# Weighted sums of the first query group taken one step later, in a fused attention and mixture-of-experts kernel

## The chip, the core and the metric

One core of one Trainium2 chip. The metric is device microseconds for one execution of the whole kernel. The engines are TensorE (PE in the profile), VectorE (DVE), ScalarE (ACT), GpSimd (POOL) and SyncE (SP, which issues DMAs here). Each runs its own list of instructions in order; semaphores tie the lists together.

## What is computed

The input `x` is 2 x 1024 tokens of width 256, the context 2 x 77 rows of width 256. The first half is a cross-attention in which every head of 16 has its own query part of a projected row, and keys and values come from context rows chosen by an argmax; the second half is a top-2 mixture of 8 experts.

```python
qp = einsum('bld,ed->ble', q, Wq);  scores = einsum('bld,bmd->blm', qp, kv)
mem = take_along_axis(kv, argmax(scores)[..., None], axis=1)
mk, mv = split(einsum('bld,ed->ble', mem, Wkv), 2)
attn = softmax(einsum('bhld,bmd->bhlm', qh, mk) * scale)
x = x + einsum('bld,ed->ble', heads(einsum('bhlm,bmd->bhld', attn, mv)), Wc)
# then, on layernorm(x): probs = softmax(x @ router_w.T); top 2 of 8 experts
h = einsum('td,eid->tei', x, w1);  y = h[..., 512:] * silu(h[..., :512])
out = x + einsum('tei,ehi,te->th', y, w2, combine)
```

Since `mem` repeats the 77 context rows, the kernel works with the 77 distinct keys and weights each by how often it was chosen (`cc`, and `vc` = values times counts).

## The kernel before

The tokens are 16 tiles of 128, in four groups of four tiles (`NH` = 4, `u` is the group). After a head that normalises x, projects queries and picks the context rows, the attention runs over the groups, and each group has four steps `s` (`STEPS`), one for four heads, written as eight slots `k` (`SLOTS`). For one step:

- TensorE, `scores_turned(u, s)` (L1405): the logits with keys on partitions, less the row maxima, into PSUM banks 0 to 3 (16 products). It waits for the exponential of the step before, which reads these banks.
- ScalarE, `exps(u, s)` (L623): the exponential of these banks into `pT`, which has two buffers.
- TensorE, `sums(u, s)` (L1421): the product of `pT` with `vc` into one bank (4 for groups 0 to 2): weighted sums and denominators. It waits for the exponential of its own step and, since there is one bank, for the normalisation of the step before. Ahead of it `fill(4, 2)` issues two products whose result nobody reads (L1273), in group 0 only.
- ScalarE, `sums_out` (L630): a copy to `uT`; TensorE, `turn_sums` (L1429): the transpose back; VectorE, `normalise` (L875, L877): reciprocal and product into `on`, which releases the next `sums`.

In between, for the group to come, TensorE computes `logits` (L1365), two per step, with tokens on partitions, and VectorE reduces each to maxima (`maxima`, L861). In groups 1 to 3 they have one pair of banks, so a logit waits for the reduction of the one before. `ahead(u, k)` names the logit that a slot of group u works on; `LEAD` = 2 puts it ten slots ahead. `turn_maxima` (L1382) and `maxima_turned` (L616) turn a whole group's maxima. `counts(1)` (L1342, L1345) counts the picks of the second batch element, and `picked`, `replaced`, `spread` on VectorE build the keys `kb` and values `vc` of it, which groups 2 and 3 need. From group 1 on, a slot also holds the steps of the group before: `turn_heads`, `combine`, `residual`, router and ranks.

A second stream runs under it. The expert weights are 48 tiles of 128 x 512. For each, a cast to the high part (`high`, L602, on ScalarE, in numbers per slot from `HIGH_SLOT`; the last few on GpSimd, L496) and the low part as a difference in bfloat16 on GpSimd (`splits`, L502) into `low`, a staging tile with `LR` = 3 buffers, 128 KB each. SyncE stores each to DRAM (`keep_lows`, L389) and loads them back when the queries' space is free (`inner_lows`, L410; the loads for experts 0 and 1 in group 1, 2 and 3 in group 2, 4 to 7 in group 3). Three waits tie the stream:

```python
if n >= 2:
    act.wait_ge(low_ok, n - 1)                        # cast of tile n: tile n-2 is subtracted
...
if n >= LR:
    pool.wait_ge(low_out[n % LR], 16 * (n // LR))     # tile n's difference: tile n-3 is stored
...
sp.wait_ge(low_ok, n + 1)                             # store of tile n
sp.dma_start(lows[n], low[:, n % LR, :]).then_inc(low_out[n % LR], 16)
```

SyncE's list is in order too. Between its stores stand other transfers, at places that `high_before(u, k)` computes from `HIGH_SLOT`: it is the number of tiles that ScalarE has cast before slot k of group u. `keep_until(n)` stores all tiles below n. `HIGH_ACT`, 45 before, is how many tiles ScalarE casts. GpSimd's list holds all 48 differences, and then the first four `gather`s (L525), which bring the rows of the first expert blocks; TensorE's `turn_rows` (L1618) waits for the first of them, and the expert products (L1633, L1642, L1649) follow. 39 blocks are worked in turn. The end of SyncE's list around it:

```python
keep_until(high_before(3, 0)); inner_lows(4); inner_lows(5)
keep_rows(1)
inner_lows(6); inner_lows(7)      # the last waits for scores(3, 3)
keep_until(NC)
sp.wait_ge(g_in[0], 16)           # the first gather
outer_lows(0); outer_lows(1)
```

Of the kernel before, what the change touches and what calls it, by code (L numbers as in the profile page):

```python
# [25 lines left out]
NH = T // HT  # L26
# [31 lines left out]
STEPS = 4  # L58
# [6 lines left out]
WC_AT = ((5, 5, 5, 5), (5, 5, 5, 5), (5, 5, 5, 7), (5, 7, 5, 7))  # L65
LEAD = 2
KB = 8
CHAIN = 7

HIGH_HEAD = (0, 0, 2, 3, 2)  # L70
HIGH_SLOT = ((2, 2, 2, 1, 2, 1, 1, 1), (2, 2, 2, 2, 2, 1, 1, 1), (2, 2, 2, 2, 2, 1, 1, 1))
HIGH_FIRST = sum(HIGH_HEAD)
# [3 lines left out]
def ahead(u, k):  # L76

    w, n = divmod(SLOTS * (u + 1) + k + LEAD, SLOTS)
    return (w, n) if w < NH else None


# [26 lines left out]
def build(nc, x, ctxT, Wq, WqT, WkvT, Wc, WcT, routerT, w, out):  # L108
    rows = nc.dram_tensor("rows", [(T + 1) * P, RW], F32).ap()
    lows = nc.dram_tensor("lows", [NC, P, CW], BF16).ap()  # L110
    with ExitStack() as ctx:
# [457 lines left out]
        def _(act):  # L569
# [107 lines left out]

            for u in range(NH - 1):
                for k in range(SLOTS):
                    if k % 2 == 0:  # L680
                        exps(u, k // 2)
                    if k == 7:
                        maxima_turned(u + 1)
                    if k % 2 == 1:
                        sums_out(u, k // 2)
                    if u >= 1 and k in (1, 2):
                        heads_turned(u - 1, k - 1)
                    if u == 2 and k == 1:
                        weights(0)
                        x2_normal(0, (0, 1))  # L690
                    if u == 2 and k == 3:
                        x2_normal(0, (2, 3))
                    high(HIGH_SLOT[u][k])

# [65 lines left out]
        def _(dve):  # L760
# [360 lines left out]

            for u in range(NH - 1):
                v = u - 1
                for k in range(SLOTS):
# [8 lines left out]
                    if k % 2 == 0 and k:  # L1133
                        normalise(u, k // 2 - 1)
                    if u == 0 and k == 2:
                        picked(1)
                    if u == 0 and k == 3:
                        replaced(1)
                    if u == 0 and k == 4:
                        spread(1)  # L1140
                    if u >= 1 and k == 3:
# [125 lines left out]
        def _(pe):  # L1267
# [140 lines left out]
            def sums(u, s):  # L1408
# [6 lines left out]
                else:  # L1415
                    pe.wait_ge(ql_ok, 2 * NH)
                if u == 0:
                    fill(4, 2)
                pe.wait_ge(ex_ok, n + 1)
# [131 lines left out]

            for u in range(NH - 1):
                for k in range(SLOTS):
# [21 lines left out]
                    if u >= 1 and k == 0:  # L1575
                        turn_sums(v, STEPS - 1)
                    if u == 0 and k == 1:
                        counts(1)
                    if u >= 1 and k == 3:
# [176 lines left out]
```

## Time and profile before

| | |
|---|---|
| median of 3 runs | 355.68 us (355.19 to 356.42) |
| profiled execution: time, span | 353.84 us, 352.0 us |
| mean granted TensorE clock | 0.986 |
| TensorE busy | 323.9 us (92% of the span) |
| VectorE, ScalarE, GpSimd busy | 192.2, 211.8, 193.1 us |
| groups 0, 1, 2 (scores to scores) | 50.34 to 71.31 to 95.76 to 121.37 us |
| first expert product | 141.64 us |

The span goes from the first to the last instruction; the execution's own time has what lies around it as well. The groups are the stretches from the first score product of one group to that of the next. Busy shares are over the whole span, most of which is the experts' loop; the attention groups fill 50 to 141 us.

### The profile page before, as it was taken

The numbers are of one execution on the slowest core, as the hardware profiler recorded it, in microseconds if no ns is written. First come the engines' busy times: TensorE is split into PE (matmuls) and PEld (weight loads), VectorE is DVE, ScalarE is ACT, GpSimd is POOL, SyncE is SP. The second block draws the span as 40 slices with busy tenths as digits, with TensorE's granted clock in tenths as the row PEclk, the third lists the DMA queues.
The fourth block names the chain that finished last, engine by engine and source line by source line (L and its number), as shares of the span: only waits on it lengthen the run. The fifth ranks groups of instructions, "written<-read, shape, count | busy, mean of one in ns | idle before, by whom it ended". The sixth has DMA issues, their size and how long they took to land.

```text
span 352.0 us, 7569 instructions
## 1 busy us (share of the span) xinstructions
PE 323.9 (92%) x2324; PEld 221.7 (63%) x2325; DVE 192.2 (55%) x648; ACT 211.8 (60%) x380; POOL 193.1 (55%) x215
## 2 busy tenths in 40 slices
PE   7998989998988899999999999999999999999940
PEld 3855544454444545786767777777777777777730
DVE  3996865636769799787884333333333333333310
ACT  1927427876788693856655556666556665566620
POOL 3401637876868783656766555545555554555330
PEclk9999999999999999999999999999999999999995
DMA  8999535825254377925234432333332333333221
GB/s 239 373 386 387 189 108 163 242 78 181 76 164 151 124 226 242 299 64 153 47 92 64 73 63 49 59 52 53 61 59 34 58 61 61 61 48 51 39 30 15
DMA packets 35690, 43.77 MB, mean 124 GB/s; under 512 B 3312, under 2 KB 28272, under 8 KB 35664
## 3 DMA queue, kind: packets, MB, share of 16 engines
q1 hardware_dynamic: 27088, 32.58, 27.9%
q0 software_dynamic: 7488, 10.39, 18.3%
q10 hardware_dynamic: 1088, 0.46, 0.6%
q8 instruction: 15, 0.25, 0.3%
q14 instruction: 11, 0.09, 0.1%
HBM read 27.49 MB, written 15.93 MB: 123 GB/s over the span
## 4 chain that ended last, share of the span: by engine, by line
PE 67%; POOL 9%; DVE 7%; DMA 6%; issue 6%; ACT 3%; SPq 0%; POOLq 0%; ACTq 0%; DVEq 0%
PE ps L1633 28%; PE ps L1642 15%; POOL low L502 6%; DMA lows<-low 5%; PE ps L1649 5%; PE ps L1332 3%; PE ps L1458 2%; PE ps L1273 2%; PE ps L1618 2%; PE ps L1421 2%; PE ps L1319 2%; POOL ex L535 2%; PE ps L1405 1%; DMA out_x<-xn,idx 1%; ACT pT L623 1%
## 5 line engine op out<-in xcount | busy, mean ns | idle before, releaser
L1633 PE MATMUL ps<-W,kb 128*128 x312 | 95.9, 429 | 0.0
L502 POOL TENSOR_TENSOR low<-raw,W 128x256 bf16<-128x256 f32 x96 | 67.0, 731 | 39.4 <-ACT W L602 31.1
L542 POOL DMA_INDIRECT out_x<-xn,idx x39 | 61.8, 1585 | 46.3 <-ACT xn L721 25.4
L525 POOL DMA_INDIRECT X<-rows,idx x39 | 39.1, 1002 | 47.7 <-ACT xn L721 34.9
L1633 PEld LDWEIGHTS ps<-W,kb 128*128 128x128 f32 x312 | 56.0, 189 | 12.4
L1195 DVE TENSOR_TENSOR kb<-ps,mT 128x512 fp32r<-128x512 f32 x39 | 27.0, 692 | 58.6 <-ACT mT L733 58.5
L1191 DVE TENSOR_TENSOR uT<-uT,ps 128x512 f32<-128x512 f32 x39 | 26.8, 686 | 45.9 <-PE ps L1633 44.3
L1633 PE MATMUL ps<-W1lo,kT 128*128 x156 | 47.2, 384 | 0.0
L721 ACT ACTIVATE xn<-ps,X 128x256 f32<-128x256 f32 x39 | 18.5, 474 | 36.0 <-PE ps L1642 31.7
L711 ACT CAST kb<-ps 128x256 fp32r<-128x256 f32 x39 | 14.5, 373 | 38.0 <-PE ps L1618 34.7
L861 DVE TENSOR_REDUCE mx<-ps 128x8 f32<-128x616 f32 x32 | 25.3, 795 | 20.3 <-PE ps L1365 20.3
L623 ACT ACTIVATE pT<-ps 77x2048 f32<-77x2048 f32 x16 | 29.9, 1871 | 5.1 <-PE ps L1405 5.0
L602 ACT CAST W<-raw 128x512 fp32r<-128x512 f32 x45 | 26.8, 616 | 7.7 <-POOL low L502 7.6
L1642 PE MATMUL ps<-W,mT 128*128 x156 | 28.7, 305 | 1.1 <-ACT mT L733 0.9
L1365 PE MATMUL ps<-kb,qhl 64*128 64x308 f32 x192 | 22.1, 334 | 4.0 <-DVE mx L861 4.0
L735 ACT CAST GT<-mT 128x512 bf16<-128x512 f32 x39 | 24.1, 618 | 1.2
L727 ACT ACTIVATE uT<-ps 128x512 f32<-128x512 f32 x39 | 23.2, 595 | 2.5 <-PE ps L1633 0.2
L1642 PE MATMUL ps<-W,kb 128*128 x156 | 24.4, 279 | 0.0
L1649 PE MATMUL ps<-ident,uT 128*128 128x128 f32 x156 | 23.6, 274 | 0.7 <-DVE uT L1191 0.4
L1642 PE MATMUL ps<-pT,GT 128*128 x156 | 23.8, 275 | 0.0
L1365 PEld LDWEIGHTS ps<-kb,qhl 64*128 64x128 f32 x192 | 14.4, 185 | 14.6 <-issue 12.8
L733 ACT CAST mT<-ps 128x512 fp32r<-128x512 f32 x39 | 22.6, 579 | 1.5 <-PE ps L1649 1.4
(202 smaller groups left out, 529.2 us busy)
## 6 DMA issues: line engine op xcount, KB each, us to landing
raw<-in_w SPq DMA_DIRECT2D x6, 1536.0 KB, 17.4
lows<-low SPq DMA_DIRECT2D x48, 128.0 KB
W1lo<-lows SPq DMA_DIRECT2D x8, 512.0 KB
raw<-in_w SPq DMA_DIRECT2D x6, 512.0 KB, 3.9
rows<-xr SPq DMA_DIRECT2D x4, 528.0 KB
X<-in_x SPq DMA_DIRECT2D x4, 512.0 KB, 7.2
out_x<-X SPq DMA_DIRECT2D x4, 512.0 KB, 3.3
pT<-lows SPq DMA_DIRECT2D x8, 256.0 KB, 4.4
```

The lines of the kernel that those rows point to most:

```text
L502: op = pool.tensor_tensor(low[:, n % LR, part], raw[:, n + 2, part], W[:, n, part].bitcast(F32), ALU.subtract)
L525: pool.indirect_dma_start(out=xg[:, b % GR, :], out_offset=None, in_=rows[0:2 * QW, :] if b < EARLY else rows, in_offset=at_rows(b)).then_ ...
L542: pool.indirect_dma_start(out=out[0:2 * QW, :] if c < EARLY else out, out_offset=at_rows(c), in_=ob[:, c % GR, :], in_offset=None, compute ...
L602: act.copy(W[:, n, :], raw[:, n + 2, :]).then_inc(hi_ok, 1)
L623: act.activation(pT[0:NK, 4 * (n % 2):4 * (n % 2) + 4, :], ps[0:NK, 0:4, :], ACT.Exp).then_inc(ex_ok, 1)
L861: dve.tensor_reduce(mx[:, t, u % 2, j * 8:j * 8 + 8].rearrange("p (r h) -> p r h", r=2), ps[:, at:at + 2, 0:HT * NK].rearrange("p r (h n) ...
L1191: dve.tensor_tensor(yb, sg, ps[:, 1, :], ALU.mult).then_inc(y_ok, 1)
L1195: dve.tensor_tensor(y_lo, ps[:, 3, :], y_hi.bitcast(F32), ALU.subtract).then_inc(yl_ok, 1)
L1365: mm = pe.matmul(ps[:, at + r, 0:HT * NK], part[half_, u, j, t * P:(t + 1) * P], kb[half_, u // 2, hl].rearrange("p h n -> p (h n)"), star ...
L1633: mm = pe.matmul(ps[:, f, :], part[:, c * P:(c + 1) * P], chunk(wts, e * WC1 + (2 * c + f)), start=(k == 0 and c == 0), stop=(k == 2 and c ...
L1642: mm = pe.matmul(ps[:, 4, 0:D], part[:, c * P:(c + 1) * P], w2, start=(k == 0 and c == 0), stop=(k == 2 and c == FC - 1))
L1649: mm = pe.transpose(ps[:, 3, c * P:(c + 1) * P], yb[:, c * P:(c + 1) * P], ident[:])
```

## The change

For group 0 only (`SKEWED` = 1) the slots are replaced by four steps in another order. `sums(0, s)` and all that follows it (`turn_sums`, `sums_out`, `normalise`) move one step later: TensorE issues scores(0,1), a logit and then the sums of step 0. `sums(0, 3)` stands alone ahead of scores(1,0). The fill ahead of each `sums` of group 0 is gone. `counts(1)`, `picked`, `replaced` and `spread` change places with it. ScalarE's casts in group 0 are 11 instead of 12, in another distribution, and with that `HIGH_ACT` becomes 44 and every `high_before` of a later group is one less; GpSimd casts four tiles (44 to 47) and not three.

```diff
--- before.py
+++ after.py
@@ -64,11 +64,12 @@
 HEADS_AT = ((5, 5), (5, 5), (5, 7), (4, 6))
 WC_AT = ((5, 5, 5, 5), (5, 5, 5, 5), (5, 5, 5, 7), (5, 7, 5, 7))
 LEAD = 2
+SKEWED = 1
 KB = 8
 CHAIN = 7
 
 HIGH_HEAD = (0, 0, 2, 3, 2)
-HIGH_SLOT = ((2, 2, 2, 1, 2, 1, 1, 1), (2, 2, 2, 2, 2, 1, 1, 1), (2, 2, 2, 2, 2, 1, 1, 1))
+HIGH_SLOT = ((2, 1, 0, 3, 0, 3, 0, 2), (2, 2, 2, 2, 2, 1, 1, 1), (2, 2, 2, 2, 2, 1, 1, 1))
 HIGH_FIRST = sum(HIGH_HEAD)
 HIGH_ACT = HIGH_FIRST + sum(sum(slots) for slots in HIGH_SLOT)
 
@@ -77,6 +78,11 @@
 
     w, n = divmod(SLOTS * (u + 1) + k + LEAD, SLOTS)
     return (w, n) if w < NH else None
+
+
+def step_before(u, s):
+
+    return (u, s - 1) if s else (u - 1, STEPS - 1) if u else None
 
 
 def logit_bank(n):
@@ -675,7 +681,21 @@
                     act.activation(xn2[:, i, :], X[:, v * HT + i, :], ACT.Identity, bias=nm2[:, i:i + 1],
                                    scale=rs2[:, i:i + 1]).then_inc(xn2_ok, 1)
 
-            for u in range(NH - 1):
+            for u in range(SKEWED):
+                for t in range(STEPS):
+                    exps(u, t)
+                    high(HIGH_SLOT[u][2 * t])
+                    if step_before(u, t):
+                        sums_out(*step_before(u, t))
+                    if u and t == 1:
+                        heads_turned(u - 1, 0)
+                    if u == 0 and t == STEPS - 1:
+                        maxima_turned(1)
+                    high(HIGH_SLOT[u][2 * t + 1])
+                    if u and t == 1:
+                        heads_turned(u - 1, 1)
+            sums_out(SKEWED - 1, STEPS - 1)
+            for u in range(SKEWED, NH - 1):
                 for k in range(SLOTS):
                     if k % 2 == 0:
                         exps(u, k // 2)
@@ -1119,7 +1139,28 @@
                 link(dve.tensor_scalar(idf, tokp, 0.0, spare[:, 0:1], ALU.is_equal, ALU.mult))
                 dve.scalar_tensor_tensor(idx[:, EARLY:BLK], tokp, -1.0, idf, ALU.add, ALU.add).then_inc(idx_ok, 1)
 
-            for u in range(NH - 1):
+            for u in range(SKEWED):
+                for t in range(STEPS):
+                    maxima(*ahead(u, 2 * t))
+                    if u == 0 and t == 1:
+                        picked(1)
+                    if u == 0 and t == 2:
+                        spread(1)
+                    if u and t == 2:
+                        residual(u - 1, 0)
+                    if u and t == 3:
+                        residual(u - 1, 2)
+                    maxima(*ahead(u, 2 * t + 1))
+                    if step_before(u, t):
+                        normalise(*step_before(u, t))
+                    if u == 0 and t == 1:
+                        replaced(1)
+                    if u and t == 2:
+                        residual(u - 1, 1)
+                    if u and t == 3:
+                        residual(u - 1, 3)
+                        choose(u - 1)
+            for u in range(SKEWED, NH - 1):
                 v = u - 1
                 for k in range(SLOTS):
                     if u == 1 and k == 5:
@@ -1132,12 +1173,6 @@
                         normalise(v, STEPS - 1)
                     if k % 2 == 0 and k:
                         normalise(u, k // 2 - 1)
-                    if u == 0 and k == 2:
-                        picked(1)
-                    if u == 0 and k == 3:
-                        replaced(1)
-                    if u == 0 and k == 4:
-                        spread(1)
                     if u >= 1 and k == 3:
                         residual(v, 0)
                     if u >= 1 and k == 4:
@@ -1414,8 +1449,6 @@
                     pe.wait_ge(sl_ok, 4)
                 else:
                     pe.wait_ge(ql_ok, 2 * NH)
-                if u == 0:
-                    fill(4, 2)
                 pe.wait_ge(ex_ok, n + 1)
                 for r in range(4):
                     mm = pe.matmul(ps[r * 32:(r + 1) * 32, sums_bank(n), :], vc[:, u // 2, :], pT[0:NK, 4 * (n % 2) + r, :],
@@ -1549,7 +1582,39 @@
                 at, n = (EARLY, LATE) if g else (0, EARLY)
                 pe.matmul(ps[:, 7, 456:456 + n], tab[:], pickb[:, at:at + n], start=True, stop=True).then_inc(idx_mm, 1)
 
-            for u in range(NH - 1):
+            def skewed(u):
+
+                v = u - 1
+                for t in range(STEPS):
+                    behind = step_before(u, t)
+                    scores_turned(u, t)
+                    logits(*ahead(u, 2 * t))
+                    if behind:
+                        sums(*behind)
+                    if u == 0 and t == 0:
+                        counts(1)
+                    if u and t == 1:
+                        turn_heads(v, 0)
+                    if u and t == 2:
+                        combine(v, 0)
+                    if u and t == 3:
+                        combine(v, 2)
+                    if u == 0 and t == STEPS - 1:
+                        turn_maxima(1)
+                    logits(*ahead(u, 2 * t + 1))
+                    if behind:
+                        turn_sums(*behind)
+                    if u and t == 1:
+                        turn_heads(v, 1)
+                    if u and t == 2:
+                        combine(v, 1)
+                    if u and t == 3:
+                        combine(v, 3)
+
+            for u in range(SKEWED):
+                skewed(u)
+            sums(SKEWED - 1, STEPS - 1)
+            for u in range(SKEWED, NH - 1):
                 for k in range(SLOTS):
                     v = u - 1
                     if k == 7:
@@ -1574,8 +1639,6 @@
                         turn_sums(u, k // 2 - 1)
                     if u >= 1 and k == 0:
                         turn_sums(v, STEPS - 1)
-                    if u == 0 and k == 1:
-                        counts(1)
                     if u >= 1 and k == 3:
                         combine(v, 0)
                     if u >= 1 and k == 4:
```

## Rows read from the trace of the kernel before

**Rows 1.** The page: its first line
```profile
span 352.0 us, 7569 instructions
```

**Rows 2.** Busy time, group 0: stretch, its length, busy us (instructions) per engine, clock, DMA
```profile
50.34:71.31 20.97, 19.11 (x212) 9.46 (x212) 12.04 (x30) 15.38 (x19) 13.97 (x20) 1.00 0.58 177
```

**Rows 3.** Timeline of TensorE, group 0: start us, us, line, operands [idle <-releaser]
```profile
50.34 0.93 PE L1405 MATMUL ps<-qhl,kb 32*77 32x512 f32 x12
...
51.43 0.69 PE L1365 MATMUL ps<-kb,qhl 64*128 64x308 f32 x6
53.12 0.69 PE L1365 MATMUL ps<-kb,qhl 64*128 64x308 f32 x6 [0.99 <-DVE mx L861]
53.73 0.61 PE L1273 MATMUL ps<-tri,ones 128*128 128x512 bf16 x2
54.27 1.06 PE L1421 MATMUL ps<-pT,vc 77*32 77x512 f32 x8
...
55.94 0.92 PE L1405 MATMUL ps<-qhl,kb 32*77 32x512 f32 x12
...
67.58 0.65 PE L1429 MATMUL ps<-ident,uT 128*128 128x128 f32 x4
68.16 1.07 PE L1382 MATMUL ps<-ident,mx 128*16 128x128 f32 x32
```

**Rows 4.** Timeline of ScalarE, group 0
```profile
51.55 1.87 ACT L623 ACTIVATE pT<-ps 77x2048 f32<-77x2048 f32 x1 [1.27 <-PE ps L1405]
53.33 1.13 ACT L602 CAST W<-raw 128x512 fp32r<-128x512 f32 x2
55.40 0.58 ACT L630 COPY uT<-ps 128x512 f32<-128x512 f32 x1 [0.95 <-PE ps L1421]
```

**Rows 5.** Timeline of ScalarE, group 1
```profile
78.44 1.87 ACT L623 ACTIVATE pT<-ps 77x2048 f32<-77x2048 f32 x1
...
86.02 0.62 ACT L602 CAST W<-raw 128x512 fp32r<-128x512 f32 x1 [2.58 <-POOL low L502]
86.54 1.87 ACT L623 ACTIVATE pT<-ps 77x2048 f32<-77x2048 f32 x1
```

**Rows 6.** Timeline of GpSimd, groups 0, 1 and hand-over
```profile
54.01 5.56 POOL L502 TENSOR_TENSOR low<-raw,W 128x256 bf16<-128x256 f32 x8 [7.24 <-ACT W L602]
...
84.57 1.41 POOL L502 TENSOR_TENSOR low<-raw,W 128x256 bf16<-128x256 f32 x2 [1.79 <-DMA lows<-low]
...
136.42 1.23 POOL L525 DMA_INDIRECT X<-rows,idx  x1 [5.84 <-DVE idx L1079]
```

**Rows 7.** Timeline of TensorE's weight loads, hand-over
```profile
140.25 0.20 PEld L1618 LDWEIGHTS ps<-ident,X 128*128 128x128 f32 x2 [0.32 <-DMA X<-rows,idx]
```

**Rows 8.** Timeline of TensorE, start of group 2
```profile
97.49 0.66 PE L1429 MATMUL ps<-ident,uT 128*128 128x128 f32 x4
99.08 0.60 PE L1273 MATMUL ps<-tri,ones 128*128 128x512 bf16 x2 [0.94 <-DVE xn L877]
```

**Rows 9.** Timeline of SyncE's queue: start us, us of issuing
```profile
78.41 0.93 SPq L410 DMA_DIRECT2D W1lo<-lows  x2
...
131.18 2.17 SPq L410 DMA_DIRECT2D W1lo<-lows  x2
133.40 1.45 SPq L389 DMA_DIRECT2D lows<-low  x3
```

**Rows 10.** Chain that ended last: start us, us, what
```profile
38.12 1.69 DMA lows<-low
...
79.39 5.05 DMA lows<-low
...
142.00 2.75 PE ps L1633 x12
```

**Rows 11.** Busy time in one stretch at the kernel's end
```profile
342.00:343.00 1.00, 0.00 (x0) 0.00 (x0) 0.00 (x0) 0.00 (x0) 0.94 (x1) 0.50 0.00 0
```

**Rows 12.** Busy time in the experts' loop
```profile
200.00:300.00 100.00, 99.71 (x624) 76.08 (x622) 35.61 (x63) 61.60 (x126) 53.80 (x42) 1.00 0.35 55
```

## The prediction

> **What bounds the kernel now.** The page gives a span of 352.0 us [rows 1]. The profiled execution took 353.84 us, so 1.84 us lie outside the span; the median of the runs, 355.68, lies another 1.84 above that one. The steps below are worked in the profiled execution's times; a net shift of x makes 353.84 + x of it, and I put the same x on the median.
>
> The table of stretches comes next, cut where the scores of group 0 (50.34) and of group 1 (71.31) start. TensorE is busy 19.11 of 20.97 us there [rows 2], so the ceiling of what group 0 can give back is the 1.86 us of idle plus the fills. The timeline of TensorE shows what fills cost: one pair, 53.73 to 54.27, is 0.54 us, and there are four pairs, 2.2 us [rows 3]. Ceiling: 4.0 us.
>
> The timelines of ScalarE and GpSimd show the second stream to watch. A cast of weight tile n on ScalarE may start only when GpSimd has finished the subtraction of tile n-2, at (5.56 / 4) = 1.39 us per tile; the ScalarE engine, being in order, holds the next exponential behind such a cast. It did so at 86.02, after 2.58 us of waiting, and the exponential came at 86.54 [rows 4 to 6].
>
> Last comes the hand-over to the experts. TensorE waits there for the first gather of rows (0.32 us, at 140.25), which GpSimd issued at 136.42 [rows 6, 7]. GpSimd had then been idle for 5.84 us: its last tile ended at 130.58. So this gather has no slack against TensorE, but the tile stream has 5.8 us against the gather.
>
> **Group 0, step by step.** Durations, from start to next start [rows 3, 4]: scores 1.09; logits 0.61; sums 1.00 (54.27 to 55.27) and then counts 0.67 (to 55.94); a turn of the sums 0.58; turning the maxima 1.0 (1.07 busy, like the sums' 1.06); the exponential starts 1.21 after its scores and holds ScalarE for 1.78; a cast is 0.51; the copy of the sums starts 1.13 after them (54.27, 55.40), lasts 0.58, and I let the next one start after 0.5. Logits into the same bank follow each other by at least 1.69 (51.43, 53.12): reduction plus two hand-overs.
>
> Step 0. Scores 50.34, logits 51.43, counts 52.04 (they fit in the wait), logits 53.12, end 53.73. The exponential ends at 53.42, so scores(0,1) go at 53.73 and not at 55.94: 2.2 us ahead. This is the change's effect, and now it is eaten.
>
> Step 1. ScalarE now has three casts ahead of the second exponential. The third, tile 9, needs tile 7 subtracted; GpSimd starts that at 54.01 [rows 6] and ends it at 55.42. Cast 9 to 56.0; exponential 56.0 and not 54.94, copy of the sums 57.78, turn 58.4, scores(0,2) 59.0. Step 2. Casts 10 to 12 follow; the last waits for tile 10 (started 58.9, ended 60.3), exponential 60.9, copy 62.7, turn 63.3, scores(0,3) 63.9. Step 3. Casts to tile 15 end 65.8, exponential 65.8, copy 67.6; logits, sums, maxima and logits fill TensorE to 68.26; turn 68.26. Then sums(0,3) stand alone: they need the normalisation of that turn. The same sequence (turn, with a reduction ahead of the normalisation) took 1.59 us in group 2, 97.49 to 99.08 [rows 8]. So sums(0,3) 69.85 and scores(1,0) 70.84, before 71.31: **0.5 us gained** of 4.0. The last term is an exact wait; the casts' ones are good to some 0.3 each.
>
> The fills' removal costs nothing of its own: nobody reads them. VectorE does the same 12.04 us of work in the stretch [rows 2] in another order; picked, replaced and spread end about 63.5, ahead of logits(2,0) at 65.0, which need them. The cover is that 1.5 us; beyond it they would cost one for one. The counts on TensorE, 0.67, lie in the wait for the reduction (51.43 + 0.61 to 53.12); without it they would be on the path. None of the moved steps issues a DMA.
>
> **Group 1.** Group 0 now has 11 casts, not 12, so every exponential of group 1 stands behind one tile less. The second, at 78.44 before, gets 77.55: 0.5 of shift and 0.4 of the shorter wait. The third stood behind tile 26, whose cast waited on tile 24, which GpSimd started at 84.57 after 1.79 us for a DMA [rows 5, 6]. Now it stands behind tile 25, hence behind tile 23. But the loads of two blocks of lows, at 78.41 before [rows 9], go as soon as tile 19 and not tile 20 is done, at 77.5, and tile 20's store goes behind them at 78.5. With the 5.05 us that such a store took, issued at 79.39 right behind the pair [rows 9, 10], it lands at 83.5, tile 23 ends at 84.95, its follower's cast at 85.46. Exponential 85.46 and not 86.54: a total of **1.1 us ahead**. From there TensorE, VectorE and ScalarE go on as a chain and pass it on; ScalarE's own idle stretches and GpSimd's leave it alone. Bounds of the gain: 0.3 (only part of group 0's) to 1.9 (no DMA wait in group 1, 0.5 more from group 0); a gain of nothing is rival C.
>
> **What comes due later.** The count of 11 also moves numbers computed from it: ScalarE casts 44 tiles in all, GpSimd casts four, not three; and SyncE's "keep until" ahead of group 3's loads stops after tile 43, not 44. Tile 44's store now stands in SyncE's last batch, behind the rows of group 1, and behind the load that waits for the last scores. Those loads take SyncE from 131.18 for 2.17 us with the wait; the batch starts at 133.40 [rows 9]. The staging has three buffers, so GpSimd can't subtract tile 47 before tile 44's store has landed. Before, tiles 45 to 47 alone were in this batch, and none of them waited for it: GpSimd was through at 130.58. Queued behind tile 47 on GpSimd is the gather, behind it TensorE and all experts.
>
> Price. Landing: the nearest row is the 5.05 us of a store issued 0.98 us after the first of two such loads (78.41, 79.39) [rows 9, 10]; here it is 2.22 after, so 5.05 - 1.24 = 3.8, and 4.0 with the store of group 1's rows in front. Ends: 1.69 us, the quickest row, and 5.05 [rows 10]. Then 0.15 to start, 1.39 for the tile, 0.1: gather at 133.40 + 4.0 + 1.65 = 139.05, before 136.42. It needed 140.25 - 136.42 = 3.8 us to reach TensorE, beside the traffic of those loads; with them gone I take 3.3 (lower end 2.9: its own 1.23 of issue and the quickest 1.69) [rows 6, 7, 10]. TensorE 142.4 and not 140.25: **2.15 us lost**. Ends: 133.40 + 1.69 + 1.65 + 2.9 = 139.6, nothing lost, and 133.40 + 5.05 + 1.65 + 3.8 = 143.9, 3.6 lost. GpSimd's fourth cast (about 0.6) is inside the wait. SyncE's loads of the second lows shift with the gather, as does everything that reads them. After that TensorE is the bound (99.71 of 100 us busy from 200 to 300, [rows 12]), so nothing is caught up.
>
> The row says that stores behind loads are slow: 5.05 us against 1.69. The Trainium skill (DMA: Bandwidth & Descriptors, Queues, rings and completion order) says why it may be so: a completion increment lands only after every earlier write of its DMA engine. By the same page's fit (about 2.0 us plus size, Anatomy of one DMA), 128 KB would be an estimated 2.3 us, tile 44 would land at 135.7, and the loss would be about 0.45 and not 2.15. This trace disagrees with the fit where loads stand in front, and the measurement decides.
>
> **Sum.** -1.1 + 2.15 = +1.05: 355.68 + 1.05 = 356.7. Its own range: with 3.2 to 4.6 for the landing and 3.1 to 3.5 for the gather the loss is 1.15 to 2.95, so -1.9 + 1.15 = -0.75 (354.9) to -0.3 + 2.95 = +2.65 (358.3).
>
> **Rivals.** (A) Faster: tile 44's store lands in about 1.7 us and the gather needs 2.9; the stall is gone and the shift stays, 355.68 - 1.1 = 354.6, with 1.9 it would be 353.8. For it: the loads may be drained by then. Against: only one of the rows is that quick. It decides once the landing is under 2.0 us. (B) The stall is about 0.5 to 1.1 us and cancels the gain: 355.1 to 355.7. (C) Group 0 and 1 give nothing, because the casts hold every exponential one tile longer than I have it, and the stall is there in full: 357.8. Against: the wait of 0.99 us and the fills are really gone. (D) TensorE's clock. At the end of the kernel, when TensorE had no product left, the granted clock was 0.50 at 342 to 343 [rows 11]: down from 2.4 to 1.2 GHz. A stall of 2 to 3 us at 140 would, if it gets there, have the first 2.75 us of expert products [rows 10] run twice as long: 356.7 + 2.7 = 359.4. The removed fills don't bring it alone: the longest wait left in group 0 is about 1.3 us, and the whole of the stretch before, with its wait of 0.99 us, stands at 1.00 [rows 2, 3].
>
> **Chances.** Forecast 0.45, A 0.24, B 0.14, C 0.11, D 0.06. A measurement of this kernel tells about 0.3% (1.07 us) from no change. The forecast sits on that edge: 0.27 of it slower, 0.18 same. A: 0.17 faster, 0.07 same. B: 0.11 same, 0.03 faster. C: 0.10 slower, 0.01 same. D: slower. Faster 0.20, same 0.37, slower 0.43. Range 354.5 to 358.6: it takes in A's centre and C, leaves out D and the far parts of A.
>
> **What would show it.** Scores(0,1) at 53.7, scores(1,0) near 70.8, the third exponential of group 1 near 85.5. GpSimd idle for several us ahead of its last tile, released by the DMA of lows; TensorE idle for about 2 us ahead of the first turned rows, released by the gather. Wrong if the last tile is done before 135, or if group 0 ends before 70 or after 71.3.

## The result and the profile after

The changed kernel takes 357.74 us (median of 8 runs, 356.85 to 359.56); the kernel before, on the same chip, 354.98 (8 runs, 352.97 to 356.42). The ratio is 1.0102 [1.0069, 1.0135]: slower, by 2.8 us in the medians and by 3.6 if the ratio is taken of 354.98. The ratios leave out executions more than 1.5% above the quickest of their kernel, which the medians include (below, 2 of 7 for e11_old_order and one each for e4_nofill, e5_filled_wait and e12_gap_casts). The forecast was +1.05. The profiled execution after took 357.77 us with a span of 356.0, 4.0 more than the span of before [rows 1]; of these 4.0, some 1.1 are there because the profiled execution of before was a quick one (353.84 against its median of 354.98).

The page of the kernel after (busy us and share of each engine; the granted clock in 40 slices, where the two 8s are slices with a stretch at the lower level):

```profile
span 356.0 us, 7537 instructions
PE 323.5 (91%) x2296; PEld 223.2 (63%) x2317; DVE 192.7 (54%) x648; ACT 211.2 (59%) x379; POOL 193.9 (54%) x216
...
PEclk9999999989999999899999999999999999999995
```

TensorE has 28 matmul records fewer than before (2296 against 2324) and is busy only 0.4 us less by time (323.5 against 323.9). With the same 2296 and no low clock, in e6_twelve below, it is 320.7; here part of them ran at 1.2 GHz. The timeline of TensorE after, group 0 and the start of group 1, against [rows 3]:

```profile
50.23 0.93 PE L1440 MATMUL ps<-qhl,kb 32*77 32x512 f32 x12
...
53.63 0.93 PE L1440 MATMUL ps<-qhl,kb 32*77 32x512 f32 x12
...
58.29 0.66 PE L1462 MATMUL ps<-ident,uT 128*128 128x128 f32 x4 [1.18 <-ACT uT L636]
58.88 0.92 PE L1440 MATMUL ps<-qhl,kb 32*77 32x512 f32 x12
...
63.79 0.94 PE L1440 MATMUL ps<-qhl,kb 32*77 32x512 f32 x12
...
70.00 1.06 PE L1454 MATMUL ps<-pT,vc 77*32 77x512 f32 x8 [0.81 <-DVE xn L897]
71.00 1.34 PE L1440 MATMUL ps<-qhl,kb 32*77 32x512 f32 x12
```

The scores come at 53.63, 58.88, 63.79 and 71.00, within 0.2 us of the forecast's 53.7, 59.0, 63.9 and 70.84. But a lead of 2.3 us at the second scores (55.94 before) is 0.3 at the next group's. What ate it stands in the timeline of ScalarE after, against [rows 4]:

```profile
53.22 1.13 ACT L608 CAST W<-raw 128x512 fp32r<-128x512 f32 x2
55.37 0.62 ACT L608 CAST W<-raw 128x512 fp32r<-128x512 f32 x1 [1.03 <-POOL low L508]
55.90 1.87 ACT L629 ACTIVATE pT<-ps 77x2048 f32<-77x2048 f32 x1
...
86.15 0.62 ACT L608 CAST W<-raw 128x512 fp32r<-128x512 f32 x1 [2.27 <-POOL low L508]
86.68 1.87 ACT L629 ACTIVATE pT<-ps 77x2048 f32<-77x2048 f32 x1
```

The third cast ahead of an exponential waits 1.03 us for GpSimd's subtraction here, and 1.43 us in step 2, and the exponential, the copy and the turn behind it wait too. In group 1 the third exponential comes at 86.68 and not at the forecast 85.46; before it was at 86.54 [rows 5].

The table by stretches after (group 0, group 1, then single microseconds; columns as in [rows 2]: length, busy time of each engine, granted clock, DMA share, GB/s):

```profile
50.23:71.00 20.77, 17.15 (x205) 9.14 (x205) 12.76 (x30) 15.09 (x19) 14.00 (x20) 1.00 0.55 172
71.00:95.91 24.91, 23.88 (x227) 13.36 (x223) 14.55 (x51) 17.72 (x24) 18.40 (x28) 0.93 0.34 112
71.00:72.00 1.00, 1.00 (x16) 0.73 (x16) 0.00 (x0) 0.59 (x1) 0.16 (x1) 0.65 0.20 68
...
142.00:143.00 1.00, 0.14 (x1) 0.15 (x2) 0.00 (x0) 0.00 (x0) 0.70 (x2) 0.99 0.25 85
143.00:144.00 1.00, 1.00 (x6) 1.00 (x6) 0.03 (x1) 0.41 (x2) 0.69 (x2) 0.50 0.43 118
144.00:145.00 1.00, 1.00 (x7) 0.94 (x6) 1.00 (x4) 0.95 (x2) 0.75 (x1) 0.50 0.93 287
```

Group 0 is 0.20 us shorter (20.77 against 20.97), group 1 is 0.46 longer (24.91 against 24.45), with the clock at its lower level from 71 to 75 us. And the clock is at 0.50 again right behind the wait at the hand-over.

That hand-over, in the timelines of GpSimd and of SyncE's queue after, against [rows 6, 9]:

```profile
130.67 0.60 POOL L502 CAST W<-raw 128x512 fp32r<-128x512 f32 x1
138.14 1.42 POOL L508 TENSOR_TENSOR low<-raw,W 128x256 bf16<-128x256 f32 x2 [6.87 <-DMA lows<-low]
139.75 1.23 POOL L531 DMA_INDIRECT X<-rows,idx  x1 [0.19 <-issue]
```

```profile
131.32 2.17 SPq L416 DMA_DIRECT2D W1lo<-lows  x2
133.54 6.36 SPq L395 DMA_DIRECT2D lows<-low  x4
```

The last batch of stores has four tiles and not three; its first is tile 44. GpSimd is idle for 6.87 us in front of tile 47, released by the landing of that store, and the gather is queued behind it. The chain that ended last runs through exactly these pieces:

```profile
133.54 4.46 DMA lows<-low
...
139.75 3.07 DMA X<-rows,idx
```

And TensorE's timeline, first before (its turned rows start at 140.25, [rows 7]), then after:

```profile
138.40 1.95 PE L1458 MATMUL ps<-WC,oT 128*128 128x264 f32 x8
...
144.58 0.38 PE L1618 MATMUL ps<-ident,X 128*128 128x128 f32 x2
```

```profile
138.54 1.95 PE L1491 MATMUL ps<-WC,oT 128*128 128x264 f32 x8
142.86 0.61 PE L1681 MATMUL ps<-ident,X 128*128 128x128 f32 x2 [2.37 <-DMA X<-rows,idx]
143.26 1.91 PE L1475 MATMUL ps<-ident,xn 128*128 128x128 f32 x8
...
148.85 0.38 PE L1681 MATMUL ps<-ident,X 128*128 128x128 f32 x2
```

The turn of eight heads' rows takes 1.91 us here and 1.04 before. I use two times below: the first turned rows (142.86, before 140.25) tell of the wait, and the distance to the second turned rows (5.99, before 144.58 - 140.25 = 4.33) tells of the clock. In this pair of profiles: arrival of TensorE at the hand-over +0.14 (138.54 against 138.40), the wait +2.47, the lower clock +1.66, sum 4.27 at the second turned rows.

### The profile page after: what moved, and what is told of

Same layout as the page of the kernel before. It is cut to its first block, busy times and chain, and to the rows that moved or that the text cites. A ratio compares the mean times of both kernels' runs of the same rounds, so it can differ in the third digit from the quotient of the medians.

```text
span 356.0 us, 7537 instructions
## 1 busy us (share of the span) xinstructions
PE 323.5 (91%) x2296; PEld 223.2 (63%) x2317; DVE 192.7 (54%) x648; ACT 211.2 (59%) x379; POOL 193.9 (54%) x216
## 4 chain that ended last, share of the span: by engine, by line
PE 71%; issue 6%; POOL 5%; DMA 5%; ACT 5%; DVE 5%; SPq 0%; POOLq 0%; ACTq 0%; DVEq 0%
PE ps L1696 28%; PE ps L1705 14%; PE ps L1712 4%; DMA lows<-low 3%; PE ps L1440 3%; PE ps L1367 3%; PE ps L1491 3%; POOL low L508 3%; PE ps L1454 3%; PE ps L1681 2%; PE ps L1308 2%; ACT pT L629 2%; PE ps L1354 2%; POOL ex L541 2%; PE ps L1400 2%
## 5 line engine op out<-in xcount | busy, mean ns | idle before, releaser
L1696 PE MATMUL ps<-W1lo,kT 128*128 x136 | 42.7, 383 | 1.3
L608 ACT CAST W<-raw 128x512 fp32r<-128x512 f32 x44 | 26.0, 618 | 8.8 <-POOL low L508 8.5
```

Of the source, the lines that this page charges most:

```text
L608: act.copy(W[:, n, :], raw[:, n + 2, :]).then_inc(hi_ok, 1)
L1696: mm = pe.matmul(ps[:, f, :], part[:, c * P:(c + 1) * P], chunk(wts, e * WC1 + (2 * c + f)), start=(k == 0 and c == 0), stop=(k == 2 and c ...
```

## The experiments

All were timed in five rounds beside the kernel before on the same chip; e1 to e4, e5 to e8, e9 to e11 and e12 were four sessions on four chips, and the changed kernel itself was in none of them. So a ratio compares with the kernel before of its own session, and two ratios of different sessions compare only through it. "Group 0" is the time from scores(0,0) to scores(1,0) in the profile, "rows" the first turned rows, "wait" TensorE's idle time ahead of them (for before, e4, e6 and e8, where the products' own row shows none, that of their weight load, which is longer by some 0.4: 2.78 and not 2.37 for the kernel after), "second" the distance to the second ones, all in us. "Low clock" names where, behind 52 us, the granted clock fell to 0.50; it came back after 3 to 4 us, and after nearly 7 us in e8_light.

| kernel | median, before | ratio [95%] | group 0 | rows | wait | second | low clock |
|---|---|---|---|---|---|---|---|
| before | 354.98 | | 20.97 | 140.25 | 0.32 | 4.33 | none |
| after | 357.74, 354.98 | 1.0102 [1.0069, 1.0135] | 20.77 | 142.86 | 2.37 | 5.99 | 71, 143 |
| e3_count | 358.99, 355.05 | 1.0092 [1.0044, 1.014] | 21.01 | 145.06 | 3.20 | 5.93 | 145 |
| e1_store44 | 355.83, 355.05 | 1.002 [0.9973, 1.0067] | 20.99 | 142.40 | 0.97 | 4.33 | 60 |
| e2_fills | 358.29, 355.05 | 1.0104 [1.0055, 1.0153] | 21.43 | 142.66 | 2.18 | 5.96 | 143 |
| e4_nofill | 357.38, 355.05 | 1.0041 [0.9992, 1.0089] | 20.14 | 143.75 | 0.35 | 4.33 | 83 |
| e5_filled_wait | 356.72, 355.67 | 1.0032 [0.9994, 1.007] | 20.37 | 143.99 | 1.03 | 4.33 | none |
| e6_twelve | 354.90, 355.67 | 0.9979 [0.9945, 1.0013] | 20.54 | 140.11 | 0.40 | 4.33 | none |
| e7_twelve_fills | 355.34, 355.67 | 0.998 [0.9947, 1.0012] | 21.45 | 141.75 | 1.04 | 4.33 | none |
| e8_light | 357.98, 355.67 | 1.0073 [1.0033, 1.0113] | 18.78 | 145.05 | 0.48 | 4.32 | 108 |
| e9_late_casts | 354.90, 354.63 | 1.0009 [0.9985, 1.0032] | 18.77 | 140.42 | 1.55 | 4.33 | none |
| e10_late_fills | 356.50, 354.63 | 1.0051 [1.0021, 1.0081] | 20.49 | 142.39 | 1.60 | 4.33 | none |
| e11_old_order | 360.26, 354.63 | 1.0112 [1.0065, 1.0159] | 19.15 | 145.75 | 1.71 | 4.34 | 91 |
| e12_gap_casts | 354.68, 355.52 | 0.9974 [0.9942, 1.0006] | 18.77 | 139.64 | 0.53 | 4.32 | none |

### Is the loss the place of tile 44's store?

**e3_count**: the kernel before, with one cast less in group 0 and nothing else.

```diff
-HIGH_SLOT = ((2, 2, 2, 1, 2, 1, 1, 1), ...
+HIGH_SLOT = ((2, 2, 2, 1, 2, 1, 1, 0), ...
```

> The kernel before with one cast less in group 0 (11, the last slot has none), nothing else: tile 44's store falls behind the last loads, as in the changed kernel. Theory: GpSimd waits about 6.5 us ahead of its last tile, TensorE 2.0 to 2.8 us ahead of the first turned rows, the clock falls there; 357.5 to 359 us as a median. Rival 1 (the new order costs): no change beyond 0.3 percent from the kernel before.

Measured: 1.0092 [1.0044, 1.014]. The old order with the new count has a loss that can't be told from the changed kernel's. Its GpSimd waits for the same store, its TensorE for the same gather, both longer than expected (timelines of both):

```profile
140.42 1.41 POOL L502 TENSOR_TENSOR low<-raw,W 128x256 bf16<-128x256 f32 x2 [7.78 <-DMA lows<-low]
...
145.06 0.44 PE L1618 MATMUL ps<-ident,X 128*128 128x128 f32 x2 [3.20 <-DMA X<-rows,idx]
```

**e1_store44**: the changed kernel, with tile 44's store ahead of group 3's loads again.

```diff
-            keep_until(high_before(3, 0))
+            keep_until(high_before(3, 0) + 1)
```

> The changed kernel with one number altered in SyncE's list: tile 44's store goes ahead of group 3's loads again, as before the change. Theory (the store's place costs 2.5 us of waiting at the hand-over and a low TensorE clock 1.7 more): GpSimd's last tile ends near 132.7 and waits for no DMA, the first gather is issued near 136.5, TensorE waits under 0.5 us for it, the clock stays at 1.00 from 140 to 148; 353.5 to 354.5 us as a median, against 357.7. Rival 1 (the new order of group 0 is what costs, through the clock at 71 to 74.5 us): the median stays at 356.5 or more. Rival 2 (the wait alone, the clock falls anyway): 355.2.

Measured: 1.002 [0.9973, 1.0067]. GpSimd now ends its four last tiles without a DMA wait, and the gather is bound by its indices again (timeline of GpSimd):

```profile
132.30 1.43 POOL L508 TENSOR_TENSOR low<-raw,W 128x256 bf16<-128x256 f32 x2
137.50 1.23 POOL L531 DMA_INDIRECT X<-rows,idx  x1 [3.77 <-DVE idx L1099]
```

The median, 355.83, is above the expected 353.5 to 354.5, and the interval leaves room for a rest of up to 0.7%. The profile shows a wait of 0.97 us and not under 0.5, and a clock that fell at 60 us.

**e6_twelve**: the changed kernel with the old count: one more cast in the last slot of group 0, `(2, 1, 0, 3, 0, 3, 0, 3)`.

> The changed kernel with twelve casts in group 0 (one more in its last slot), so that all numbers computed from the count are those of before: the new order and the missing products alone. Theory (the count is the whole loss, the order is worth nothing): within 0.3 percent of the kernel before, no DMA wait over 2 us ahead of GpSimd's last tile; group 0 takes 20.8 to 21.2 us. Rival (the order itself costs): slower than before by 0.5 percent.

Measured: 0.9979 [0.9945, 1.0013], with a wait of 0.40 us at the hand-over and no low clock. So both ways of giving tile 44's store its place back remove the loss or most of it, and e1_store44 moves nothing but that store. e3_count, in the old order, brings the loss; it takes the place away, but also gives GpSimd a fourth cast, which e1_store44 has too without the loss. What is left of the order itself is too small to be told from nothing.

### The clock in the wait

**e5_filled_wait**: the changed kernel, with eight products that nobody reads issued in the wait.

```diff
+            fill(0, 8)
             turn_rows(0, 16)
```

> The changed kernel with eight unused products (2.2 us) ahead of the first turned rows, that is in TensorE's wait for the gather. If the low clock from 143 to 147 us comes from that wait, it stays at 1.00 there and the way from the first turned rows to the second (6.0 us in the changed kernel, 4.33 before) shortens to about 4.3: 1.5 us less, 356.2 as a median against 357.7. The wait for tile 44's store stays (over 6 us on GpSimd). Rival: the products push the turned rows back or the clock falls anyway; 357.5 or more.

Measured: 1.0032 [0.9994, 1.007]. GpSimd waits as in the changed kernel (7.26 us for the store), the gather is as late, but the clock stays up (timeline of TensorE, then the table by stretches):

```profile
141.07 1.89 PE L1308 MATMUL ps<-tri,ones 128*128 128x512 bf16 x8
143.99 0.44 PE L1681 MATMUL ps<-ident,X 128*128 128x128 f32 x2 [1.03 <-DMA X<-rows,idx]
144.27 1.04 PE L1475 MATMUL ps<-ident,xn 128*128 128x128 f32 x8
```

```profile
144.00:145.00 1.00, 1.00 (x9) 1.00 (x10) 0.07 (x1) 0.45 (x2) 0.69 (x2) 1.00 0.52 137
```

The second turned rows follow after 4.33 us and not 5.99. So of the loss in the pair of before and after, 1.66 us is the clock behind the wait, shown by holding the wait and filling it. The time agrees in sense (expected 356.2, measured 356.72), but its interval just touches the changed kernel's. In the study's profiles the clock fell right behind the three unfilled hand-over waits of 2.18, 2.37 and 3.20 us, and behind none of those of 1.71 us or less. Three more waits for an exponential fit this: 1.86 us in e4_nofill, 2.29 in e8_light and 1.84 in e11_old_order, each with the lower clock within 1.4 us behind it. These six are all of TensorE's waits of 1.84 us or more behind its first product in the 14 profiles. The reverse doesn't hold: the clock also fell behind shorter ones.

### Do the removed fills matter?

**e4_nofill**: the kernel before, without the fills.

```diff
-                if u == 0:
-                    fill(4, 2)
```

> The kernel before without the unused products of group 0, in the old order. Theory: they lie partly on the path, scores of group 1 start 0.5 to 1.5 us earlier, the waits for the reductions take the rest; if the clock falls near 70 us without them too, this is given back by group 1. Median 354 to 355.5 against 355.0. Rival 1 (the low clock belongs to the new order alone): the clock stays at 1.00 and the gain of about 1 us stays in the total.

**e2_fills**: the changed kernel with these two lines put back. **e7_twelve_fills**: e6_twelve with them.

> The changed kernel with the two unused products ahead of each weighted sum of group 0 put back. Theory: in group 0 the clock stays at 1.00 from 71 to 75 us, the scores of group 1 start 0.2 to 0.6 us later than without them but the first sums of group 1 earlier (75 and not 75.7); the hand-over's wait of 2.4 us and its low clock stay, so the median is 357 to 358. Rival 1 (the new order of group 0 costs): the median falls to 355.5 or less.

> As the one with twelve casts, with the two unused products ahead of each weighted sum of group 0 put back: the new order alone. Theory: group 0 takes 21.3 to 21.7 us, against 20.97 before (the order costs about 0.5), and the clock stays at 1.00 from 60 to 76 us; total 0 to 0.4 percent slower than before. Rival (the products only cost): slower than its twin without them by their 0.5 us.

Measured: group 0 is 20.14 and not 20.97 without them in the old order, and 21.43 and 21.45 with them in the new one, against 20.77 and 20.54. So the fills hold 0.7 to 0.9 us of group 0, of the 2.2 they are long. In time this is worth nothing that can be measured: e4_nofill 1.0041 [0.9992, 1.0089], e7_twelve_fills 0.998 [0.9947, 1.0012] beside e6_twelve's 0.9979. And e2_fills, at 1.0104 [1.0055, 1.0153], has the whole loss: putting them back cures nothing at the hand-over.

One reason why e4_nofill gains nothing is in its group 1. There GpSimd waits 3.66 us for a store (2.81 before), the casts ahead of the second exponential wait for GpSimd, and TensorE waits 1.86 us for that exponential (0.70 before); then the clock falls (timeline of TensorE, then the table by stretches):

```profile
82.80 1.13 PE L1419 MATMUL ps<-pT,vc 77*32 77x512 f32 x8 [1.86 <-ACT pT L623]
```

```profile
83.00:84.00 1.00, 1.00 (x9) 0.14 (x1) 0.00 (x0) 1.00 (x3) 0.28 (x1) 0.83 1.12 370
84.00:85.00 1.00, 1.00 (x3) 0.79 (x4) 0.00 (x0) 0.65 (x2) 1.00 (x2) 0.50 0.97 225
```

Group 1 lasted 27.44 us there, against 24.45. Between 52 and 130 us the clock fell in 5 of the 9 profiles without fills (after, e1, e4, e8, e11) and in none of the 5 with them (before, e2, e3, e7, e10). That seems to point to the fills, but in three of the five (e4, e8, e11) it fell behind one of the long waits named above, outside group 0. Only after (at 71) and e1 (at 60) had no such wait; the waits they had there, 0.81 and 1.17 us, stand in e5 and e6 too, without a fall. And four of the five (all but after) are among the six profiles in which the clock had already fallen in the head, told of in the last section. What brought the falls in after and e1 stays open.

### What is the order worth?

**e8_light**: the changed kernel with 8 casts in group 0, none of which has to wait, and four more in group 2.

```diff
+HIGH_SLOT = ((2, 0, 0, 2, 0, 2, 0, 2), (2, 2, 2, 2, 2, 1, 1, 1), (3, 3, 3, 3, 2, 1, 1, 1))
```

> The changed kernel with eight casts in group 0, placed so that no exponential stands behind a cast that waits for GpSimd (2 after the first exponential, 2 after each copy), and four more in group 2; 45 on ScalarE, so tile 44's store is early. Theory (the casts hold the exponentials and eat the new order's gain): the exponentials of group 0 start 1.2 us after their scores, group 0 takes 19.0 to 19.6 us, 1.4 to 2 us less than 20.97. In the total 353.5 to 354.5 if group 1 and 2 carry it, unless the tiles run late. Rival (the normalisation's chain sets group 0 whatever the casts do): 20.5 us or more.

Measured: group 0 drops to 18.78, a little below the expected range, and yet 1.0073 [1.0033, 1.0113], with a median of 357.98 where 353.5 to 354.5 were expected. It is given back in group 2, where scores(2,1) and scores(2,2) are 9.96 us apart and not 6.83, by a wait of 2.29 us and the lower clock behind it (timelines of ScalarE and TensorE):

```profile
105.10 0.62 ACT L608 CAST W<-raw 128x512 fp32r<-128x512 f32 x1 [1.00 <-POOL low L508]
105.63 1.87 ACT L629 ACTIVATE pT<-ps 77x2048 f32<-77x2048 f32 x1
...
107.64 1.60 PE L1454 MATMUL ps<-pT,vc 77*32 77x512 f32 x8 [2.29 <-ACT pT L629]
```

**e9_late_casts**: the same light group 0, the usual groups 1 and 2, the last seven casts on GpSimd, and tile 44's store ahead of the rows of group 1.

```diff
+HIGH_SLOT = ((2, 0, 0, 2, 0, 2, 0, 2), (2, 2, 2, 2, 2, 1, 1, 1), (2, 2, 2, 2, 2, 1, 1, 1))
...
+            keep_until(45)
             keep_rows(1)
```

> The changed kernel with eight casts in group 0, as in the light one, but the four that are left over done by GpSimd at the end (seven there), and SyncE storing tile 44 ahead of group 1's rows. Theory: group 0 takes 18.8 us, groups 1 and 2 as before (24.5 and 25.6), GpSimd's last tile ends by 134.5 and the first gather is issued near 134.5, TensorE waits under 1 us for it: 1.5 to 2 us less than the kernel before in a profile without a low clock, ratio 0.993 to 0.998. Rival: the long row of tiles on GpSimd makes the gather late and the gain goes there; ratio 1.000 or more.

Measured: 1.0009 [0.9985, 1.0032]; the rival's ratio, 1.000 or more, is what came. Group 0 is 18.77, groups 1 and 2 keep their length (24.44, 25.62), and then GpSimd is late itself, with no wait between its last tile and the gather, which goes at 136.84 and not near 134.5 (table by stretches of group 0, then the timeline of GpSimd):

```profile
50.35:69.12 18.77, 16.97 (x204) 9.12 (x205) 11.99 (x30) 13.63 (x16) 10.32 (x15) 1.00 0.41 127
...
136.84 1.23 POOL L532 DMA_INDIRECT X<-rows,idx  x1 [0.19 <-issue]
```

**e10_late_fills** is e9_late_casts with the fills, and **e11_old_order** is the kernel before without fills, with the casts and the store of e9_late_casts: the order of sums and scores, with the casts and the steps for the second batch element in their places around it, is all that tells it from e9_late_casts.

> As the one with seven late casts, with the two unused products ahead of each weighted sum of group 0 put back. If the products guard the clock, no low clock from 50 to 80 us and group 0 of 19.3 to 20.0 us; ratio 0.993 to 1.000, with a smaller spread than its twin. If they only cost, 0.5 to 1 us slower than the twin.

> The kernel before in its old order, without the unused products, with the same eight casts in group 0, seven late ones and the same place of tile 44's store: what the new order itself is worth once the casts are out of the way. Theory: the old order has the exponential of a step ahead of its own sums, so group 0 takes 19.8 to 20.3 us (20.1 with the casts of before), 1.0 to 1.5 more than the new order's 18.8. Rival (the casts were the whole matter): 19.0 us or less here too.

Measured: group 0 is 19.15 in the old order and 18.77 in the new one. So the order that this change is named after is worth 0.4 us there, by one profile each; the expected 19.8 to 20.3 was wrong, and the rival's 19.0 was nearer. The rest, 1.6 to 2.0 us (20.37 in e5_filled_wait and 20.77 in after, which are the same program up to there, against 18.77), is the casts, above all the three that wait for GpSimd. The 0.4 us between these two is also what one execution differs from another, so the 0.2 us between before and after is within it. In time e11_old_order takes longest of all, 1.0112 [1.0065, 1.0159]. Its profile has a wait for an exponential in group 1, a lower clock at 91 to 95 behind it (group 1 lasted 27.83 us), and a late gather, so its ratio doesn't weigh the order (timeline of TensorE):

```profile
89.98 1.06 PE L1420 MATMUL ps<-pT,vc 77*32 77x512 f32 x8 [1.84 <-ACT pT L624]
```

With fills the light group 0 is 20.49, above the expected 19.3 to 20.0, and 1.0051 [1.0021, 1.0081]: once no cast waits, the fills cost 1.7 us of their 2.2.

**e12_gap_casts**: e9_late_casts with one cast more in group 0's last slot and two more in group 2, so that GpSimd casts four tiles again.

```diff
+HIGH_SLOT = ((2, 0, 0, 2, 0, 2, 0, 3), (2, 2, 2, 2, 2, 1, 1, 1), (2, 2, 2, 2, 2, 2, 2, 1))
```

> As the one with seven late casts, but nine in group 0 and two more in group 2's slots 5 and 6, where ScalarE waits 2.2 us before the last exponential; GpSimd has four late casts, as in the changed kernel. Theory: group 0 stays at 18.8 to 19.0 us, group 2 at 25.6 to 26.0, GpSimd's last tile ends 1.5 to 2 us earlier than with seven late casts, and the first turned rows start at 138.5 to 139.3 from a start of group 0 at 50.3 (140.25 before); ratio 0.993 to 0.998. Rival (group 0's gain always comes back as a late tile stream): first turned rows at 140 or later, ratio 0.999 or more.

Measured: 0.9974 [0.9942, 1.0006]. In the profile the gather is early enough (135.42, released by its indices), and scores(0,0) to first turned rows is 89.04 us against 89.91 before; but group 2 has grown from 25.61 to 26.26, and the first turned rows at 139.64 are later than the expected 138.5 to 139.3. It, e6_twelve and e7_twelve_fills are the best of the study, and none is shown to beat the kernel before.

## Why the prediction was partly right and partly wrong

- **Group 0** (0.5 gained): 0.20 in the profiled pair, 0.60 with e5_filled_wait in place of after, with the scores within 0.2 us of the forecast's. Right in mechanism: the casts eat the lead, and e9_late_casts shows it, since it gives back 2.0 us when no cast waits.
- **Group 1** ("a total of 1.1 us ahead"): this step failed. The load pair went at 78.61, not at 77.5, the third exponential came at 86.68, not 85.46, and TensorE reached the hand-over 0.14 us later than before and not 1.1 earlier. Two things stand in its place. The first is the clock, which the forecast had at 1.00: the chain that ended last runs through TensorE and its short turns with VectorE here, and not through the tile stream, with scores(1,0) at the lower level at its head (the third exponential, done at 88.55, would have held TensorE's next sums, at 88.69, almost as long).

```profile
71.07 1.70 PE ps L1440 x13
```

e5_filled_wait is the same program up to there and kept its clock. Counted from scores(0,0), its third exponential comes after 35.77 us and its hand-over after 87.65; before it was 36.20 and 88.06, after 36.45 and 88.31. So with the clock up the program is 0.4 us ahead, and in the profiled pair 0.25 behind. Between after and e5_filled_wait 0.40 us were lost in group 0 already, with the clock up in both, and 0.29 in group 1, where the clock of after was low.

The second is that even at full clock the lead is 0.4 and not 1.1 us. From scores(1,0) to the third exponential it is 15.40 us in e5_filled_wait and 15.23 before; the forecast had 14.62. The chain there hangs on the store behind the load pair, tile 20's, whose landing took longer than the 5.05 us that the forecast carried over (the chain in e5_filled_wait):

```profile
79.99 5.32 DMA lows<-low
...
85.44 1.42 POOL low L508 x2
...
87.41 1.88 ACT pT L629
```

And the cast that group 0 lacks is one that GpSimd lacks. The timeline of GpSimd after, at the start of group 1:

```profile
71.84 1.41 POOL L508 TENSOR_TENSOR low<-raw,W 128x256 bf16<-128x256 f32 x2 [0.86 <-DMA lows<-low]
75.27 2.81 POOL L508 TENSOR_TENSOR low<-raw,W 128x256 bf16<-128x256 f32 x4 [2.02 <-ACT W L608]
```

It does one tile and stands idle for 2.02 us (1.84 in e5_filled_wait): tile 18 is cast only behind the first exponential of group 1 (at 74.59). Before, the twelfth cast ran at 71.93, ahead of that exponential, and GpSimd worked from 72.32 without a break for 8.32 us. But giving that cast back, in e6_twelve, gains nothing either: 15.37 us to the third exponential, behind a store that landed in 5.28. How much the idle time alone costs was not shown.
- **The hand-over** (2.15 lost): this was right. Landing 4.46 us against the 4.0 taken (4.85 and 5.35 in e5_filled_wait and e3_count), gather 139.75 against 139.05, gather to TensorE 3.07 against 3.3, the wait 2.47 longer. e3_count, e1_store44 and e6_twelve show that the place of one store decides it. By the fit of the Trainium skill (DMA: Bandwidth & Descriptors, Anatomy of one DMA), which is one for transfers that GpSimd issues, the landing would have been an estimated 2.3 us. The median of all 48 such stores in this trace is near it, 2.1 us; this one, with loads in front, took 4.46, and the measurement decides.
- **Clock**: the second step that failed, left out of the sum at nothing. Rival D, at 0.06, named it, and its place was right: it fell behind the wait, for 1.66 us and not 2.7, and e5_filled_wait took it away. That a wait of this length is enough was not to be read from the trace of before, whose only row of it was the end of the kernel, but it deserved far more than 0.06, and the forecast's own 2.15 us stall should have carried it. "The removed fills don't bring it alone" is neither shown nor refuted: the clock also fell at 71 in this profile, after a group 0 whose longest wait was 1.18 us. In e4_nofill, where the fills are all that is gone, it fell too, but behind a wait of 1.86 us in group 1.

The sum again with what the profiles measured: arrival at the hand-over +0.14 instead of -1.1, wait +2.47 instead of +2.15, clock +1.66 instead of 0. That is 4.27 of the profiled pair. The medians differ by 2.76, since the executions differ. The forecast of +1.05 was too low by the first and the third term. Slower was its likeliest side, for the right reason. That the time lay within its range is in part luck: the change, 2.76 us, is above the +2.65 at the upper end of the sum's own range, and the kernel before came out 0.7 us quicker than the 355.68 from which the range was counted.

## What to carry to other kernels

A number that is used for work (how many casts a slot has) may also be used for a position (which stores stand ahead of a load in an in-order list). Follow every use of it: here the second use, one store behind five transfers and a ring of three buffers, cost most or all of what the kernel lost, and the reordering nothing that could be measured. Before crediting a stage with less work, ask whether that work was feeding another engine. And when a forecast puts a wait of some 2 us on a TensorE that was busy until then, add a stretch at the lower clock behind it: all six waits of 1.84 to 3.20 us had one, and at the hand-over it cost 1.6 us. Products that nobody reads, issued in such a wait, took it away (e5_filled_wait).

## What was not expected of the hardware

The clock also differs from one execution to the next in places where the programs are the same. In six profiles (e1, e3, e4, e5, e8, e11) it fell in the head, ahead of group 0, and scores(0,0) came at 51.56 to 51.80 and not at 50.15 to 50.60; here e1_store44, whose head is that of the kernel after (table by stretches):

```profile
48.00:49.00 1.00, 1.00 (x4) 0.25 (x4) 0.00 (x0) 0.00 (x0) 0.00 (x0) 0.50 0.75 249
```

That is some 1.3 us of difference between executions. I take it to be one part of the spread of the medians' runs (before: 352.97 to 359.18 over all sessions); this is argued and not shown. What decides whether it falls was not found.
